# Conditioned residual block on one core: TensorE, VectorE and ScalarE take parts of a step in another order

## The chip, the cores and the metric

The kernel runs on one core of a Trainium2 chip. The time is device microseconds of one launch; the figure for a kernel is the median over its runs.

## The reference, cut to what matters

Two residual layers over x of 2 batches x 2048 rows x 512 features, all float32:

```
x1  = x + x @ W(mu) + bias(mu)      W(mu) = U(mu) @ V, rank 30, one per batch
xn  = norm(x1)                      rows to mean 0, variance 1
h   = norm(xn*pw_g[path] + pw_b[path]) * cp_g[cls] + cp_b[cls]
t   = xn * tm_g[cls] + tm_b[cls]
s   = xn * ms_g[scale] + ms_b[scale]
m,n,r = x1 + three vectors of the batch (from small MLPs of the conditions)
hid = concat(w0 h, w1 t, w2 m, w3 n, w4 r, w5 s) @ int_W1 + b1
y   = x1 + norm(silu(hid) @ int_W2 + b2) * g + be
```

## The kernel before

The 4096 rows are 32 tiles of 128 rows. A head loads and prepares the weights: it decodes U from W_dec, splits every weight into a high part in TensorE's reduced format and the low remainder, and runs the x part of `hid` for twelve tiles (2 to 13, "kept") ahead of time, while W_dec streams in; these results wait in `stash`. Then comes one step per tile.

Each product of 128x512 with a 512x512 weight is three matmuls for each of four chunks (high x high, high x low, low x high), 12 matmuls of 512 columns, in `product` (L743 to L745). What a product needs is first transposed by TensorE (`transpose`, L737, four 128x128 blocks), then copied out of the bank as its high part by ScalarE (`split_hi`, L591) and subtracted for its low part by VectorE (`split_lo`, L1244).

In step n five tiles are in work: a = n+2, f = n+1, m = n, c = n-1, b = n-2. TensorE does, in this order: the x product of m (not for kept tiles, L961), `expand` of f (L804, gives x @ W for x1), the transposes of h of m, `low_rank` of m (L809, the m, n, r parts and the rank part of hid), the t product of m, the transposes of z = silu(hid) of c, the s product of m, the second product of c (with W2, operand `zop`), `offsets` of m (L813, the class offsets by a one-hot matrix), the transposes of t and of s of f, `embed` of a (L794) and the h product of m. A kept step has 51 matmuls of 512 columns, a later one ("ring step", after the ring in which x is loaded) 63.

VectorE sums x1 of f (`first_sum`, L1276), for a kept c adds the stashed x part to hid (L1443, into z), takes x1's statistics (`x_stats`, L1249 and L1253), adds the bias to the output of b and takes its statistics (`out_stats`), multiplies xn by the gains of t (`scaled`, L1288) and s (`scale_rows`, L1296), splits z (`z_split`, L1244), scales the output of b (L1370), splits h, takes h's statistics, finishes b's rows (L1378), splits s, makes the stack for the next expand (`stacked`), the one-hot matrix (L1212), h's class product (`h_gain`, L1305) and splits t. ScalarE applies silu to c (L604 for a kept c, L609 else), makes the high part of x of a (`x_high`, L562), normalises x (`x_norm`, L640), copies z's and h's high parts, then s's, `embedded`, normalises h and copies t's. GpSimd turns variances into factors (L1021, L1029, L1034), subtracts x's low part (`x_low`, L1070), gathers gains by indirect DMA and does h's pathway gain. SyncE issues the loads; for kept tiles x comes to `xraw` (L405).

The order on each engine is written out by hand in the `step` functions; an engine takes its instructions in that order, and the engines meet at semaphores. The steps 15 to 26 are a loop of three rounds of four; the rest is unrolled.

Of the kernel before, what the change touches and what calls it, by code (L numbers as in the profile page):

```python
# [106 lines left out]
def kept(t):  # L107

    return t.i is None and PRE0 <= t.s < PRE0 + NPRE


def ringed(t):

    return t.exists() and not kept(t) and t.s >= PRE0 + NPRE
# [13 lines left out]
def build(nc, d, out):  # L128
# [11 lines left out]
    with ExitStack() as ctx:  # L140
# [369 lines left out]
        def _(act):  # L510
# [40 lines left out]
            def x_high(a):  # L551
                s = a.slot
                old = a.plus(-2)
                if ringed(a):
                    act.wait_ge(stash_in[a.row], ring_count(a))
                    if kept(old):
                        act.wait_ge(xu_ready, old.count())
                    else:
                        act.wait_ge(x_free, old.count())
                else:  # L560
                    act.wait_ge(xT_in[s], a.slot_count(16))
                nc.scalar.activation(xop[:, s, HI, :, :], x_rows(a), ACT.Copy).then_inc(x_hi, 1)  # L562
# [38 lines left out]
            def silu(m):  # L601
                if kept(m):
                    act.wait_ge(z_whole, m.s - PRE0 + 1)
                    nc.scalar.activation(z[:, :], z[:, :], ACT.Silu, bias=0.0).then_inc(z_ready, 1)  # L604
                else:
                    act.wait_ge(hid_ready, m.count())
                    if is_first(m):
                        act.wait_ge(x_used, 1)
                    nc.scalar.activation(z[:, :], HID[m.slot][:, :], ACT.Silu, bias=0.0).then_inc(z_ready, 1)  # L609
# [75 lines left out]

            def step(n):
                a, f, m, c, b = n.plus(2), n.plus(1), n, n.plus(-1), n.plus(-2)
                silu(c)
                if kept(n):
                    x_high(a)  # L690
                if f.exists():
                    x_norm(f)
                z_high(c)
                if m.exists():
                    h_high(m)
                if a.exists() and not kept(n):
                    x_high(a)
                if f.exists():
                    s_high(f)
                if a.exists():  # L700
                    embedded(a)
                if f.exists():
                    h_norm(f)
                    t_high(f)
# [18 lines left out]
        def _(pe):  # L723
# [82 lines left out]
            def low_rank(m):  # L806
                if kept(m):
                    pe.wait_ge(z_ready, m.count(extra=-1))
                return nc.tensor.matmul(HID[m.slot][:, :], stack_of(m), VWst[:, :], start=kept(m), stop=False)  # L809

            def offsets(m):
                pe.wait_ge(oh_ready, m.count())
                nc.tensor.matmul(HID[m.slot][:, :], OH[:, m.slot, :], BT[:, :], start=False, stop=is_first(m)) \  # L813
                    .then_inc(x_used, 1)
# [7 lines left out]
            def transpose_s(m):  # L822
                pe.wait_ge(s_ready, m.count())
                if m.plus(-1).exists():
                    pe.wait_ge(h_lo, m.count(extra=0))
                transpose(TP[1], st, sT)

            def transpose_h(m):
                pe.wait_ge(h_ready, m.count())
                pe.wait_ge(s_lo, m.count())  # L830
                transpose(TP[1], ht, hT)
# [125 lines left out]
            def step(n):  # L957
                a, f, m, c, b = n.plus(2), n.plus(1), n, n.plus(-1), n.plus(-2)
                if m.exists() and not kept(m):
                    pe.wait_ge(z_ready, m.count(extra=-1))  # L960
                    product(HID[m.slot], xop[:, m.slot, :, :, :], W1[:, X, :, :, :], True, False)  # L961
                if f.exists():
                    expand(f)
                if m.exists():
                    transpose_h(m)
                    low_rank(m).then_inc(x_free, 1)
                if kept(m):
                    t_product(m, FRONT)
                if m.exists():
                    t_product(m, BACK if kept(m) else range(KC))  # L970
                transpose_z(c)
                if m.exists():
                    s_product(m)
                if not is_last(m):
                    second_product(c)
                if m.exists():
                    offsets(m)
                if f.exists():
                    transpose_t(f)
                    transpose_s(f)  # L980
                if a.exists():
                    embed(a)
                if m.exists():
                    h_product(m)
# [165 lines left out]
        def _(v):  # L1150
# [107 lines left out]
            def stacked(f):  # L1258
                v.wait_ge(inner_part, f.count())
                nc.vector.tensor_tensor(inner[:, :], inner[:, :], XU[:, P:2 * P], ALU.add).then_inc(inner_ready, 1)  # L1260
                v.wait_ge(inner_ready, f.count())
                if f.plus(-3).exists():
                    v.wait_ge(x_used, f.count(extra=-1))
                dst = stack_of(f)
                nc.vector.tensor_copy(dst[:, :], inner[:, :]).then_inc(stack_part, 1)
                v.wait_ge(stack_part, f.count())
                nc.vector.tensor_tensor(dst[2 * Q:3 * Q, :], inner[2 * Q:3 * Q, :], dst[2 * Q:3 * Q, :].bitcast(F32),
                                        ALU.subtract).then_inc(stack_ready, 1)

            def first_sum(f):  # L1270
                s = f.slot
                v.wait_ge(xv_ready, f.count())
                v.wait_ge(x0_in[s], f.slot_count(16))
                if f.plus(-2).exists():
                    v.wait_ge(xb_ready, f.count(extra=-1))
                nc.vector.tensor_tensor(x1[:, s, :], XV[:, :], x0[:, s, :], ALU.add).then_inc(x1_ready, 1)  # L1276

            def x_stats(f):
                v.wait_ge(x1_ready, f.count())
                stats(0, x1[:, f.slot, :], f, 0, mv1_ready)  # L1280

            def scaled(f):
                m, s = f.plus(-1), f.slot
                v.wait_ge(xhat_ready, f.count())
                v.wait_ge(ct_in[s], f.slot_count(16))
                if m.exists():
                    v.wait_ge(tT, m.count())
                nc.vector.tensor_tensor(tt[:, :], xhat[:, :], ctt[:, s, D:2 * D], ALU.mult).then_inc(t_ready, 1)  # L1288

            def scale_rows(f):  # L1290
                m, s = f.plus(-1), f.slot
                v.wait_ge(xhat_ready, f.count())
                v.wait_ge(sg_in[s], f.slot_count(16))
                if m.exists():
                    v.wait_ge(sT, m.count())
                nc.vector.tensor_tensor(st[:, :], xhat[:, :], sgt[:, s, :], ALU.mult).then_inc(s_ready, 1)  # L1296
# [6 lines left out]
            def h_gain(f):  # L1303
                v.wait_ge(hn_ready, f.count())
                nc.vector.tensor_tensor(ht[:, :], ht[:, :], ctt[:, f.slot, 0:D], ALU.mult).then_inc(h_ready, 1)  # L1305
# [130 lines left out]
            def step(n):  # L1436
                a, f, m, c, b = n.plus(2), n.plus(1), n, n.plus(-1), n.plus(-2)
                if f.exists():
                    first_sum(f)
                if c.exists() and kept(c):  # L1440
                    v.wait_ge(hid_ready, c.count())
                    v.wait_ge(zT, c.count(extra=0))
                    nc.vector.tensor_tensor(z[:, :], HID[c.slot][:, :], stash[:, c.s - PRE0, :],  # L1443
                                            ALU.add).then_inc(z_whole, 1)
                if f.exists():
                    x_stats(f)
                out_stats(b)
                if f.exists():
                    scaled(f)
                    scale_rows(f)  # L1450
                z_split(c)
                out_scaled(b)
                if m.exists():
                    h_split(m)
                if f.exists():
                    h_stats(f)
                out_row(b)
                if f.exists():
                    s_split(f)
                if a.exists():  # L1460
                    stacked(a)
                    one_hot(a)
                if f.exists():
                    h_gain(f)
                    t_split(f)

            for n in range(2, FIRST):
# [133 lines left out]
```

## Time and profile before

| what | value |
|---|---|
| median of 3 runs | 621.7 us (621.47 to 622.83) |
| the profiled execution | 621.03 us |
| its span | 619.2 us |
| PE / PEld busy | 588.5 / 452.8 us |
| DVE / ACT / POOL busy | 418.3 / 200.1 / 391.1 us |
| granted TensorE clock | 0.997 of full speed |

The span is what the trace covers; 1.8 us of the execution lie outside it. PE is TensorE's matmuls, PEld its weight loads, DVE VectorE, ACT ScalarE, POOL GpSimd. Matmuls are pipelined: a matmul's own duration overlaps the next one, so the distance between two starts is what it costs.

### The profile page before, as it was taken

How to read it: one execution, taken by the hardware profiler on the slowest of the kernel's cores; microseconds unless marked ns; L12 is line 12 of the kernel's file. 1: busy time of each engine (PE TensorE's matmuls, PEld its weight loads, DVE VectorE, ACT ScalarE, POOL GpSimd, SP SyncE). 2: the span in 40 equal slices, each digit the busy share in tenths (PEclk: the TensorE clock that was granted, in tenths of full speed). 3: DMA queues.
4: the chain of work that ended last, by engine and by line, in shares of the span. 5: the costliest groups of instructions: out<-in, count | busy, mean ns of one | idle time of the engine just before them, and what ended most of it. 6: DMA issues, size and time to landing. Idle time of an engine off the chain costs nothing.

```text
span 619.2 us, 9159 instructions
## 1 busy us (share of the span) xinstructions
PE 588.5 (95%) x2924; PEld 452.8 (73%) x2924; DVE 418.3 (68%) x750; ACT 200.1 (32%) x346; POOL 391.1 (63%) x499
## 2 busy tenths in 40 slices
PE   0899899999999999999999999999999999999995
PEld 0455346588888888888888888888888888888784
DVE  3511378588888888888676667766666666667744
ACT  3333354433333334333232332333223322332222
POOL 1002457568888888888766766666777666666720
PEclk9999999999999999999999999999999999999998
DMA  8999997424554445545524444454433434444201
GB/s 290 405 403 379 325 344 266 128 87 140 157 158 141 141 148 162 162 153 153 147 100 124 133 141 125 122 140 140 140 123 103 134 121 122 132 140 104 88 19 51
DMA packets 53119, 102.07 MB, mean 165 GB/s; under 512 B 10446, under 2 KB 23246, under 8 KB 52956
## 3 DMA queue, kind: packets, MB, share of 16 engines
q1 hardware_dynamic: 39872, 58.52, 27.7%
q0 software_dynamic: 12160, 42.04, 22.6%
q10 hardware_dynamic: 1052, 1.07, 0.5%
q8 instruction: 18, 0.29, 0.2%
q14 instruction: 17, 0.14, 0.1%
HBM read 93.10 MB, written 8.39 MB: 164 GB/s over the span
## 4 chain that ended last, share of the span: by engine, by line
PE 78%; DMA 6%; DVE 5%; issue 3%; POOL 3%; ACT 2%; SPq 1%; ACTq 0%; DVEq 0%; POOLq 0%
PE bank L743 21%; PE bank L745 21%; PE bank L744 21%; PE bank L737 8%; DMA ring<-in_W_dec 4%; PE bank L794 2%; PE bank L731 2%; SPq L332 1%; DMA Uf<-Ur 1%; PE bank L813 1%; PE bank L809 1%; PE bank L804 1%; DVE bn L1249 1%; POOL rs L1029 1%; DMA pwt<-in_pw,idx 1%
## 5 line engine op out<-in xcount | busy, mean ns | idle before, releaser
L743 PE MATMUL bank<-W,ops 128*128 128x512 f32 x432 | 175.4, 406 | 0.0
L745 PE MATMUL bank<-W,ops 128*128 128x512 f32 x432 | 171.0, 396 | 0.0
L744 PE MATMUL bank<-W,ops 128*128 128x512 f32 x432 | 170.9, 396 | 0.0
L591 ACT ACTIVATE ops<-bank 128x512 fp32r<-128x512 f32 x97 | 57.1, 590 | 158.1 <-PE bank L737 158.1
L743 PEld LDWEIGHTS bank<-W,ops 128*128 128x128 f32 x432 | 81.6, 189 | 25.6 <-issue 8.6
L745 PEld LDWEIGHTS bank<-W,ops 128*128 128x128 f32 x432 | 81.3, 188 | 19.6
L744 PEld LDWEIGHTS bank<-W,ops 128*128 128x128 f32 x432 | 81.6, 189 | 16.1
L1244 DVE TENSOR_TENSOR ops<-bank,ops 128x512 fp32r<-128x512 f32 x97 | 66.2, 683 | 14.1 <-ACT ops L591 14.1
L1249 DVE BATCH_NORM_STATS2 bn<-h 128x6 f32<-128x512 f32 x32 | 22.2, 692 | 55.2 <-POOL h L1081 55.2
L1021 POOL TENSOR_SCALAR ve<-mv 128x1 f32<-128x1 f32 x94 | 31.6, 336 | 42.9 <-DVE mv L1253 40.4
L640 ACT ACTIVATE xhat<-x,nm,rs 128x512 f32<-128x512 f32 x32 | 26.1, 816 | 94.1 <-POOL nm L1034 94.1
L743 PE MATMUL bank<-W,zop 128*128 128x512 f32 x124 | 50.7, 409 | 0.7 <-DVE zop L1244 0.4
L1081 POOL TENSOR_TENSOR h<-h,pwt 128x512 f32<-128x512 f32 x32 | 47.5, 1484 | 2.5
L744 PE MATMUL bank<-W,zop 128*128 128x512 f32 x124 | 49.0, 395 | 0.0
L745 PE MATMUL bank<-W,zop 128*128 128x512 f32 x124 | 48.9, 395 | 0.0
L1070 POOL TENSOR_TENSOR xop<-stash,xop 128x512 fp32r<-128x512 f32 x18 | 23.3, 1293 | 39.4 <-ACT xop L562 39.4
L1370 DVE SCALAR_TENSOR_TENSOR o<-o,mv,gbc 128x512 f32<-128x512 f32 x31 | 47.5, 1531 | 0.0
L1046 POOL DMA_INDIRECT ctt<-in_ct,idx x32 | 40.3, 1258 | 7.7 <-issue 6.4
L1079 POOL TENSOR_TENSOR h<-xhat,pwt 128x512 f32<-128x512 f32 x32 | 42.7, 1334 | 2.9 <-ACT xhat L640 1.9
L647 ACT ACTIVATE ht<-h,nm,rs 128x512 f32<-128x512 f32 x32 | 26.1, 816 | 56.1 <-POOL nm L1034 56.1
L332 POOL DMA_DIRECT2D Uf<-Ur x12 | 6.5, 564 | 58.4 <-ACT Ur L548 58.4
L1090 POOL TENSOR_TENSOR xb<-x,bebc 128x512 f32<-128x512 f32 x32 | 42.3, 1323 | 0.6
(145 smaller groups left out, 1084.5 us busy)
## 6 DMA issues: line engine op xcount, KB each, us to landing
ring<-in_W_dec SPq DMA_DIRECT2D x16, 960.0 KB, 12.1
x<-in_x SPq DMA_DIRECT2D x32, 256.0 KB
out<-xb SPq DMA_DIRECT2D x31, 256.0 KB
stash<-in_xT SPq DMA_DIRECT2D x30, 256.0 KB, 6.2
ring<-in_int_W SPq DMA_DIRECT2D x4, 1024.0 KB, 9.8
xraw<-in_xT SPq DMA_DIRECT2D x14, 256.0 KB
mnr<-in_int_W SPq DMA_DIRECT2D x12, 256.0 KB, 8.2
idxrep<-in_rows SPq DMA_DIRECT2D x64, 32.0 KB
```

What stands on the lines that cost most here:

```text
L591: nc.scalar.activation(dst.rearrange("p c t -> p (c t)"), bank[:, :], ACT.Copy).then_inc(done, 1)
L737: last = nc.tensor.transpose(dst[:, c * P:(c + 1) * P], src[:, c * P:(c + 1) * P], ident)
L743: nc.tensor.matmul(bank[:, :], op[:, HI, c, :], w[:, HI, c, :], start=start and c == 0, stop=False)
L744: nc.tensor.matmul(bank[:, :], op[:, HI, c, :], w[:, LO, c, :], start=False, stop=False)
L745: last = nc.tensor.matmul(bank[:, :], op[:, LO, c, :], w[:, HI, c, :], start=False, stop=stop and c == KC - 1)
L1021: nc.gpsimd.tensor_scalar(ve[:, which:which + 1], mv[:, which, 1:2], EPS, 1.0, ALU.add, ALU.mult) \
L1046: pool.indirect_dma_start(out=dst[:, s, :], out_offset=None, in_=d[table], in_offset=bass.IndirectOffsetOnAxis(ap=idx[:, s, col:col + 1], ...
L1079: nc.gpsimd.tensor_tensor(h1[:, :], xhat[:, :], pwt[:, s, 0:D], ALU.mult).then_inc(h1_part, 1)
L1081: nc.gpsimd.tensor_tensor(h1[:, :], h1[:, :], pwt[:, s, D:2 * D], ALU.add).then_inc(h1_ready, 1)
L1090: nc.gpsimd.tensor_tensor(xb[:, f.row, :], x1[:, f.slot, :], bebc[:, :], ALU.add).then_inc(xb_ready, 1)
L1244: nc.vector.tensor_tensor(dst.rearrange("p c t -> p (c t)"), bank[:, :], hi.bitcast(F32).rearrange("p c t -> p (c t)"), ALU.subtract).then ...
L1370: nc.vector.scalar_tensor_tensor(out=o[:, :], in0=o[:, :], scalar=mv[:, 2, 0:1], in1=gbc[:, :], op0=ALU.subtract, op1=ALU.mult).then_inc(u ...
```

## The change

Nothing is added or removed; instructions change places within the step of three engines. The head written out before the first step, the loads and GpSimd's order stay.

```diff
@@ ScalarE, step @@
-                silu(c)
                 if kept(n):
                     x_high(a)
+                silu(c)
                 if f.exists():
                     x_norm(f)
                 z_high(c)
@@ TensorE, step @@
                 if f.exists():
                     expand(f)
                 if m.exists():
+                    low_rank(m).then_inc(x_free, 1)
                     transpose_h(m)
-                    low_rank(m).then_inc(x_free, 1)
...
                 if not is_last(m):
                     second_product(c)
-                if m.exists():
-                    offsets(m)
                 if f.exists():
                     transpose_t(f)
                     transpose_s(f)
+                if m.exists():
+                    offsets(m)
                 if a.exists():
                     embed(a)
@@ VectorE, step @@
                 if f.exists():
                     first_sum(f)
+                    x_stats(f)
                 if c.exists() and kept(c):
                     v.wait_ge(hid_ready, c.count())
                     v.wait_ge(zT, c.count(extra=0))
                     nc.vector.tensor_tensor(z[:, :], HID[c.slot][:, :], stash[:, c.s - PRE0, :],
                                             ALU.add).then_inc(z_whole, 1)
-                if f.exists():
-                    x_stats(f)
                 out_stats(b)
                 if f.exists():
+                    scale_rows(f)
                     scaled(f)
-                    scale_rows(f)
                 z_split(c)
...
                 if a.exists():
                     stacked(a)
+                if f.exists():
+                    h_gain(f)
+                if a.exists():
                     one_hot(a)
                 if f.exists():
-                    h_gain(f)
                     t_split(f)
```

## Rows read from the trace of the kernel before

**Rows 1.** The page's part 1: busy us, share of the span, instructions.
```profile
PE 588.5 (95%) x2924; PEld 452.8 (73%) x2924; DVE 418.3 (68%) x750; ACT 200.1 (32%) x346; POOL 391.1 (63%) x499
```
**Rows 2.** Busy time by stretch: stretch, its length, engines, clock, DMA share, GB/s.
```profile
200.00:250.00 50.00, 49.92 (x252) 40.50 (x251) 42.51 (x79) 17.45 (x31) 41.43 (x54) 1.00 0.48 151
...
400.00:450.00 50.00, 50.00 (x248) 40.98 (x247) 34.22 (x64) 14.75 (x27) 35.04 (x45) 1.00 0.46 130
```
**Rows 3.** Waits from 143 to 303 us: total us, times, longest.
```profile
PEld bank L743 <- DVE zop L1244: 5.1, 11, 0.5
```
**Rows 4.** Timeline of one kept step, TensorE: start, duration, engine, line, what, count, [idle before].
```profile
215.06 0.39 PE L813 MATMUL bank<-BT,OH 128*128 128x512 f32 x1
...
219.43 0.39 PE L804 MATMUL bank<-Vst,stack 128*128 128x512 f32 x1
...
222.88 0.59 PEld L737 LDWEIGHTS bank<-cst,z 128*128 128x128 f32 x4
...
223.12 0.60 PE L737 MATMUL bank<-cst,z 128*128 128x128 f32 x4
...
226.12 0.40 PE L745 MATMUL bank<-W,ops 128*128 128x512 f32 x1
...
226.56 0.50 PE L743 MATMUL bank<-W,zop 128*128 128x512 f32 x1
...
226.90 0.40 PE L744 MATMUL bank<-W,zop 128*128 128x512 f32 x1
...
229.46 0.40 PE L813 MATMUL bank<-BT,OH 128*128 128x512 f32 x1
```
**Rows 5.** The same step on VectorE, from x1's sum to z's split.
```profile
219.90 0.68 DVE L1276 TENSOR_TENSOR x<-bank,x 128x512 f32<-128x512 f32 x1
...
220.50 0.68 DVE L1443 TENSOR_TENSOR z<-bank,stash 128x512 f32<-128x512 f32 x1
...
221.09 0.69 DVE L1249 BATCH_NORM_STATS2 bn<-x 128x6 f32<-128x512 f32 x1
...
221.89 0.18 DVE L1253 BATCH_NORM_AGGREGATE mv<-bn 128x2 f32<-128x6 f32 x1
...
223.51 0.18 DVE L1253 BATCH_NORM_AGGREGATE mv<-bn 128x2 f32<-128x6 f32 x1
...
224.39 0.91 DVE L1288 TENSOR_TENSOR tt<-xhat,ctt 128x512 f32<-128x512 f32 x1 [0.70 <-ACT xhat L640]
...
225.23 0.68 DVE L1296 TENSOR_TENSOR st<-xhat,sgt 128x512 f32<-128x512 f32 x1
...
225.83 0.68 DVE L1244 TENSOR_TENSOR zop<-bank,zop 128x512 fp32r<-128x512 f32 x1
```
**Rows 6.** The same step on ScalarE and GpSimd, with the wait before each.
```profile
221.21 0.63 ACT L604 ACTIVATE z<-z 128x512 f32<-128x512 f32 x1 [2.15 <-DVE z L1443]
...
221.75 0.61 ACT L562 ACTIVATE xop<-xraw 128x512 fp32r<-128x512 f32 x1
...
222.23 0.19 POOL L1021 TENSOR_SCALAR ve<-mv 128x1 f32<-128x1 f32 x1 [0.48 <-DVE mv L1253]
...
223.55 0.82 ACT L640 ACTIVATE xhat<-x,nm,rs 128x512 f32<-128x512 f32 x1 [1.18 <-POOL nm L1034]
```
**Rows 7.** Timeline of a ring step on VectorE, where statistics follow x1's sum directly.
```profile
410.82 0.69 DVE L1276 TENSOR_TENSOR x<-bank,x 128x512 f32<-128x512 f32 x1 [0.55 <-PE bank L804]
...
411.55 0.70 DVE L1249 BATCH_NORM_STATS2 bn<-x 128x6 f32<-128x512 f32 x1
```
**Rows 8.** Groups by form, 160 to 600 us: busy us, mean ns, idle before.
```profile
L809 PE MATMUL bank<-VWst,stack 128*128 128x512 f32 x28 | 13.3, 475 | 0.0
...
L813 PE MATMUL bank<-BT,OH 128*128 128x512 f32 x27 | 10.6, 393 | 0.0
```
**Rows 9.** SyncE issues the load of x for the kept step.
```profile
217.02 0.43 SPq L405 DMA_DIRECT2D xraw<-in_xT  x1
```
**Rows 10.** DMA issues by line: count, KB each, median us to landing.
```profile
stash<-in_xT SPq DMA_DIRECT2D x30, 256.0 KB, 6.2
```

## The prediction

> **What bounds the kernel now.** I read the page's busy shares first, then the busy time by stretch, then the waits of the stage with the smallest margin, then one step of it on every engine. The shares say TensorE: 588.5 of 619.2 us [rows 1]. The stretches say where it could still gain: from 400 to 450 us, in the ring steps, it is busy 50.00 of 50 us, from 200 to 250 us, in the kept steps, 49.92, with VectorE at 42.5 us and GpSimd at 41.4 [rows 2]. Busy time hides what pipelining costs, so I go by starts. The waits of 143 to 303 us name one thing before the weight loads: `zop`, the low part of z, from VectorE, 11 times [rows 3].
>
> In one kept step the price can be read. Two matmuls of the second product that follow each other are 0.233 us apart. The last matmul of the s product starts at 226.12, the first that needs zop at 226.56, the next at 226.90: 0.78 us where two distances would be 0.47, so 0.31 us are lost, partly in waiting, partly because the weights of the late matmul could no longer be loaded under the one before [rows 4]. The step is 229.46 - 215.06 = 14.40 us long; without the loss it would be 14.09, and nothing else in it waits. A ring step has 12 matmuls more, 12 x 0.233 = 2.8 us in which zop gets ready, and loses nearly nothing.
>
> Why is zop late? z's split is at 225.83, behind the products for t (224.39) and s (225.23) on VectorE; the t product waited 0.70 us for xhat [rows 5]. ScalarE could start xhat only at 223.55, when GpSimd had the factor; GpSimd started at 222.23 on the statistics, which VectorE finished at 221.89 + 0.18 = 222.07 [rows 5, 6]. These statistics stood behind the sum of z with the stash (220.50), which takes VectorE's place for 0.60 us.
>
> **The change part by part.** I count from the start of `expand` of the same step, E = 219.43 [rows 4].
>
> *x's statistics before z's stash sum.* The first statistic starts today at E+1.66. Put directly behind x1's sum it needs that sum's result, and in a ring step this costs 0.73 us from start to start instead of 0.60 [rows 7]: sum at E+0.47, statistic at E+1.20, 0.46 us earlier than now. Everything on that chain moves with it: statistics done at E+2.18, GpSimd's factor begins at E+2.34, xhat at 4.12 - 0.46 = E+3.66 and ready at E+4.48. The work on VectorE between does not get less, only its idle 0.70 us shrinks: the stash sum goes to E+2.10 (0.10 behind the start of x's aggregate at E+2.00), and the output's bias and statistics, whose aggregate ends at 223.51 + 0.18 = E+4.26 now [rows 5], are pushed by the 0.13 us that x's sum and statistic lie further apart, to about E+4.40, just before xhat. So the multiplication that waits for xhat starts at E+4.50, the next after 0.84 (the first of the two takes 0.91 us, as now: GpSimd subtracts x's low part beside it) at E+5.34, z's split after 0.60 at E+5.94, done at E+6.62. z's high part is no obstacle: ScalarE can copy it as soon as xhat is through, at about E+4.4. TensorE wants zop for the matmul at 226.12 + 0.233 = E+6.92, with its weights loaded, for which I take 0.11 us (the excess of 0.34 over 0.233 between 226.56 and 226.90) [rows 4]. The low part reaches it 0.05 after VectorE's end, as today (226.51 to 226.56), so at E+6.67 against E+6.81. The stall of 0.31 us goes, with 0.14 us to spare. What is late next is the stash sum itself.
>
> *The stash sum later, silu later.* It ends at E+2.78 instead of E+1.75, silu (0.63 us) runs from E+2.81 to E+3.44, and the weight load of z's transposes, today at 222.88 = E+3.45, can take it at E+3.49. That is 0.04 late, but a load may start 0.11 before its matmul at E+3.69. So it costs nothing; the margin is under 0.1 us. This is the tightest place. Bounds: 0 if the lead holds, 0.04 to 0.10 a step if not, 0.5 to 1.2 us over twelve steps; I take 0, because the deadline is that of the matmul.
>
> *x's high part before silu on ScalarE.* Today it starts at 221.75 = E+2.32, without any wait for its load, 0.54 us after silu [rows 6]; its load was issued at 217.02 = E-2.41 [rows 9], so the landing takes at most 4.73 us. The issue hangs on the output rows of b, which are on the chain that moves 0.46 earlier while the step gets 0.31 shorter, so it comes at about E-2.56; the latest landing that the trace allows is then E+2.17, x's high part is done by E+2.8 and silu starts at E+2.81 as above. Cost 0, hidden in the wait of 2.15 us that ScalarE has before silu. What it brings is an earlier x_low operand, which nobody waits for.
>
> *s product before t product on VectorE.* Both of t and s are wanted only by the transposes after the second product, three microseconds later. Cost and gain 0.
>
> *h's class product before the one-hot matrix.* In ring steps VectorE idles before it for the normalised h anyway; the 0.29 us of the one-hot matrix then lie behind it and push t's split by up to 0.3, where VectorE afterwards idles 0.55 us [rows 7]. In kept steps t's split keeps its place, as the same work is done before it. Cost 0.
>
> *low_rank before h's transposes, offsets behind those of t and s.* The same matmuls are issued, and there are still three changes from transposes to matmuls in a step. The matmul right behind transposes lasts longer (low_rank 475 ns, offsets, behind a product, 393) [rows 8]: 0.08 us, the part of a weight load that a short transpose cannot cover. After the change the t product's first matmul and offsets stand there instead of low_rank and embed. So the same price is paid in the same number of places. I take 0; the bounds are one such exposure more or less per step, 0.08 x 30 = 2.4 us either way. The h transposes get 0.23 us more time for h; nobody waits for either moved matmul, since both add into an open sum.
>
> No DMA is moved; those of SyncE follow the same semaphores.
>
> **The sum.** Eleven kept steps x 0.31 = 3.4 us [rows 3, 4]. Ring steps, head and tail 0. The profiled execution goes from 621.03 to 617.6 us (span 619.2 to 615.8); it lies 0.7 us under the median, so the median goes from 621.7 to 618.3 us.
>
> **The rivals.**
>
> *A: silu is held up behind x's load (slower).* ScalarE takes its instructions in order. If x's load has not landed, silu waits with it, and TensorE waits at z's transposes. The median landing of the same 256 KB into stash is 6.2 us [rows 10]. At that, x lands at E+3.64, silu ends near E+4.9 and the transposes stall by about 1.4 us, in the nine kept steps (3 to 11) whose x comes through xraw: 9 x 1.4 = 12.6 us more, less the 3.4 us of the zop stall that goes, so about 631 us. It decides from a landing of 5.2 us on (x at E+2.64, silu and z 0.45 later than in my count, 0.31 us of stall behind the lead: all the gain). For it: order, and that median. Against it: all those landings took at most 4.73 us, or x's high part would have shown a wait [rows 6, 9]. The Trainium skill ("TensorE: Matmul & The Clock Gate", section "Architectural detail: the array is 16× 32×32, not 1× 128×128") says that ScalarE's and VectorE's queues are strictly first in, first out, and only weight loads are pulled ahead. The trace agrees: z's split stood behind the t product that waited 0.70 us [rows 5]. By that rule rival A has no way out once a load is late.
>
> *B: the stall only moves (no change).* The margins of 0.14 us at zop and below 0.1 at z's transposes are both differences of overlapping spans. If the stash sum, 0.9 us later than now, makes z's transposes late by 0.1 to 0.2 us, and zop is late by as much, a step keeps most of its 0.31 us: 620.0 to 621.5 us, I say 620.7. For it: VectorE's work ahead of z's split is unchanged and only 0.70 us idle can be taken from it. Against it: the counts above.
>
> The Trainium skill ("SBUF — State Buffer", section "SBUF: two separate sides") has VectorE and GpSimd lock each other out of a shared port for a whole instruction when VectorE reads two SBUF operands. The t product's 0.91 us while x_low ran fits that more or less. By the rule the first product would wait for x_low's end at about E+4.89, zop would come 0.15 us later than in my sum, and the gain would be some 0.1 us smaller in all.
>
> *C: TensorE's new neighbours cost or save an exposed weight load in each of 30 steps.* 618.3 + 2.4 = 620.7, or 618.3 - 2.4 = 615.9 us. Rows 8 speak for a fixed price per change of kind, so for neither.
>
> **How the numbers follow.** Forecast 0.66, A 0.08, B 0.14, C dearer 0.05, C cheaper 0.05, and 0.02 for slower in another way. The range takes B and the dearer C in and reaches 1.5 us below the forecast: 616.8 to 621.0; outside remain A, most of the cheaper C and little else. About 0.2%, 1.2 us, is what a measurement can tell here: faster is below 620.5, which has the forecast, the cheaper C and some of B and the dearer C, 0.79; within 0.2% the rest of these, 0.11; slower A and the rest, 0.10.
>
> **What would show it.** Right: in the kept steps no wait of the weight loads for zop, steps of 14.1 us between two `offsets`, x's statistic 0.73 us behind x1's sum, xhat 0.46 us earlier after expand, silu ending about 3.4 us after expand with z's transposes still at 3.7, ring steps unchanged at 16.9. Wrong: a wait of z's transposes for silu (B, or A if x's high part shows a wait for its load); ring steps shorter or longer by 0.08 (C).

## The result, and the profile after

The changed kernel runs in 618.68 us (median of 6, 618.12 to 619.33) against 622.12 us (median of 6) for the kernel before on the same chip: ratio 0.9946, 95% interval 0.9933 to 0.9959. That is 3.4 us less; the forecast was 3.4 us less and 618.3 us. A run that lies over 1.5% above the fastest of its kernel is left out of medians and ratios; in this document that is one run, of e9. The two profiled executions differ by 2.0 us only (spans 619.2 and 617.2 us), since in the second one the head, which waits for weights, happened to take 1.1 us longer: `expand` of step 3 starts at 148.51 us there and at 147.41 us before (in the traces of the experiments it lies anywhere from 147.9 to 150.4). From that point on the changed kernel takes 468.7 us and the old one 471.8, 3.1 us less. It lies in the eleven steps from there to `expand` of step 14: 161.26 us before, 158.10 now. A ring step is as long as before, 16.91 us against 16.90.

The page's busy line for the changed kernel [rows 1]:

```profile
PE 586.1 (95%) x2924; PEld 454.5 (74%) x2924; DVE 417.5 (68%) x750; ACT 204.2 (33%) x346; POOL 390.1 (63%) x499
```

The waits of the changed kernel from 143 to 303 us [rows 3]: the eleven waits for zop (5.1 us) are one of 0.2 us, and ScalarE now waits for x's load before it makes x's high part, which before it never did.

```profile
ACT xop L562 <- DMA xraw<-in_xT: 7.0, 9, 1.5
...
ACT xhat L640 <- POOL nm L1034: 2.5, 11, 0.3
...
PEld bank L743 <- DVE zop L1244: 0.2, 1, 0.2
```

TensorE in one kept step of the changed kernel [rows 4]; here E, the start of `expand`, is 219.09:

```profile
215.52 0.47 PE L813 MATMUL bank<-BT,OH 128*128 128x512 f32 x1
...
219.09 0.39 PE L804 MATMUL bank<-Vst,stack 128*128 128x512 f32 x1
219.33 0.39 PE L809 MATMUL bank<-VWst,stack 128*128 128x512 f32 x1
...
222.79 0.60 PE L737 MATMUL bank<-cst,z 128*128 128x128 f32 x4
...
225.79 0.40 PE L745 MATMUL bank<-W,ops 128*128 128x512 f32 x1
226.03 0.39 PE L743 MATMUL bank<-W,zop 128*128 128x512 f32 x1
226.26 0.40 PE L744 MATMUL bank<-W,zop 128*128 128x512 f32 x1
...
229.62 0.47 PE L813 MATMUL bank<-BT,OH 128*128 128x512 f32 x1
```

The first matmul that needs zop starts 0.24 us after the one before and its follower 0.23 us later, where both together took 0.78 us. The step is 14.10 us long. `low_rank`, no longer behind transposes, shows 0.39 us and `offsets`, now behind them, 0.47: the exposed weight load changed its place, as rows 8 had it.

VectorE in the same step [rows 5]: x's statistic at E+1.19, aggregate at E+1.99, stash sum at E+2.09, then s, t and z's split.

```profile
219.57 0.68 DVE L1276 TENSOR_TENSOR x<-bank,x 128x512 f32<-128x512 f32 x1
220.28 0.69 DVE L1249 BATCH_NORM_STATS2 bn<-x 128x6 f32<-128x512 f32 x1
221.08 0.18 DVE L1253 BATCH_NORM_AGGREGATE mv<-bn 128x2 f32<-128x6 f32 x1
221.18 0.69 DVE L1444 TENSOR_TENSOR z<-bank,stash 128x512 f32<-128x512 f32 x1
...
223.64 0.91 DVE L1296 TENSOR_TENSOR st<-xhat,sgt 128x512 f32<-128x512 f32 x1 [0.15 <-ACT xhat L640]
224.47 0.68 DVE L1288 TENSOR_TENSOR tt<-xhat,ctt 128x512 f32<-128x512 f32 x1
225.07 0.68 DVE L1244 TENSOR_TENSOR zop<-bank,zop 128x512 fp32r<-128x512 f32 x1
```

ScalarE and GpSimd in it [rows 6]: x's high part is done before silu may start, and nothing stands before xhat but GpSimd's factor.

```profile
220.07 0.63 ACT L562 ACTIVATE xop<-xraw 128x512 fp32r<-128x512 f32 x1 [1.45 <-DMA xraw<-in_xT]
...
221.91 0.64 ACT L604 ACTIVATE z<-z 128x512 f32<-128x512 f32 x1 [1.21 <-DVE z L1444]
...
222.72 1.28 POOL L1070 TENSOR_TENSOR xop<-xraw,xop 128x512 fp32r<-128x512 f32 x1
222.79 0.81 ACT L640 ACTIVATE xhat<-x,nm,rs 128x512 f32<-128x512 f32 x1 [0.25 <-POOL nm L1034]
```

### The profile page after: what moved, and what is told of

Same layout as the page of the kernel before. It is cut to its first block, busy times and chain, and to the rows that moved or that the text cites. A ratio compares the mean times of both kernels' runs of the same rounds, so it can differ in the third digit from the quotient of the medians.

```text
span 617.2 us, 9159 instructions
## 1 busy us (share of the span) xinstructions
PE 586.1 (95%) x2924; PEld 454.5 (74%) x2924; DVE 417.5 (68%) x750; ACT 204.2 (33%) x346; POOL 390.1 (63%) x499
## 4 chain that ended last, share of the span: by engine, by line
PE 68%; POOL 7%; issue 7%; DMA 7%; DVE 6%; SPq 2%; ACT 2%; POOLq 0%; DVEq 0%; ACTq 0%
PE bank L743 18%; PE bank L744 18%; PE bank L745 18%; PE bank L737 7%; DMA xraw<-in_xT 2%; PE bank L731 2%; DMA ring<-in_W_dec 2%; DMA ring<-in_int_W 2%; PE bank L794 2%; SPq L332 2%; DVE bn L1249 2%; POOL rs L1029 1%; POOL h L1081 1%; POOL h L1079 1%; POOL ctt L1046 1%
## 5 line engine op out<-in xcount | busy, mean ns | idle before, releaser
L744 PEld LDWEIGHTS bank<-W,ops 128*128 128x128 f32 x432 | 81.9, 190 | 14.8
L1046 POOL DMA_INDIRECT sgt<-in_ms_g,idx x32 | 35.4, 1105 | 11.4 <-issue 11.4
## 6 DMA issues: line engine op xcount, KB each, us to landing
ring<-in_W_dec SPq DMA_DIRECT2D x16, 960.0 KB, 12.5
```

The lines of the kernel that those rows point to most:

```text
L744: nc.tensor.matmul(bank[:, :], op[:, HI, c, :], w[:, LO, c, :], start=False, stop=False)
L1046: pool.indirect_dma_start(out=dst[:, s, :], out_offset=None, in_=d[table], in_offset=bass.IndirectOffsetOnAxis(ap=idx[:, s, col:col + 1], ...
```

## The experiments

Each is given with its median and its ratio to the kernel before on the same chip. All expectations count from E, as the prediction does. The third column of the table is the mean length of the eleven steps from `expand` of step 3 to that of step 14 in the trace, less the 2.80 us that the x product (12 matmuls) puts into the last of them; it leaves the head's scatter out. Single slow steps are in these means: one of 14.86 us in e1, of 14.40 in e2 and of 15.19 in e3; the medians of the eleven are 14.40, 14.10 and 14.56.

| kernel | median us, ratio (95% interval) | kept step us |
|---|---|---|
| before | 622.1 | 14.41 |
| changed | 618.68, 0.9946 (0.9933 to 0.9959) | 14.12 |
| e1, statistics only | 621.82, 0.9996 (0.9987 to 1.0005) | 14.46 |
| e2, statistics and x's high part | 619.33, 0.9954 (0.9940 to 0.9967) | 14.14 |
| e3, all but the statistics | 623.54, 1.0020 (1.0011 to 1.0029) | 14.60 |
| e5, x's high part only | 621.69, 0.9996 (0.9986 to 1.0007) | 14.40 |
| e6, TensorE's moves only | 622.07, 1.0000 (0.9992 to 1.0009) | 14.38 |
| e7, e3 with the one-hot matrix back | 622.58, 1.0008 (0.9998 to 1.0018) | 14.40 |

**e1, x's statistics before z's stash sum, nothing else.**

```diff
                 if f.exists():
                     first_sum(f)
+                    x_stats(f)
                 if c.exists() and kept(c):
...
-                if f.exists():
-                    x_stats(f)
                 out_stats(b)
```

> Before, with x's statistics put before z's stash sum on VectorE and nothing else. Theory 1, as the prediction had it (x's high part before silu is worth nothing): the whole stall at zop goes, 3.4 us faster than before, the same as the full change. Theory 2: with silu now at E+2.8 to E+3.45, x's high part, which stands behind silu here, runs until about E+4.0 and holds xhat back from E+3.7 to about E+3.9; zop comes some 0.25 us later than in the changed kernel and the matmul waits 0.1 to 0.15 us more in each kept step: only about 2 us faster than before.

Measured 621.82 us: no gain at all, less than even the second theory gave. E is 221.96 in this step of e1:

```profile
224.75 0.63 ACT L604 ACTIVATE z<-z 128x512 f32<-128x512 f32 x1 [3.18 <-DVE z L1444]
225.29 0.62 ACT L562 ACTIVATE xop<-xraw 128x512 fp32r<-128x512 f32 x1
225.81 0.80 ACT L640 ACTIVATE xhat<-x,nm,rs 128x512 f32<-128x512 f32 x1
...
225.99 1.29 POOL L1070 TENSOR_TENSOR xop<-xraw,xop 128x512 fp32r<-128x512 f32 x1 [0.36 <-ACT xop L562]
...
226.65 1.18 DVE L1288 TENSOR_TENSOR tt<-xhat,ctt 128x512 f32<-128x512 f32 x1 [0.32 <-ACT xhat L640]
...
228.36 0.68 DVE L1244 TENSOR_TENSOR zop<-bank,zop 128x512 fp32r<-128x512 f32 x1
```

Silu waits for the later stash sum and x's high part, behind it, holds up two things: xhat starts at E+3.85 where the changed kernel has E+3.70, and GpSimd's x_low at E+4.03 where it has E+3.63. The t product, which overlaps x_low, then lasts 1.18 us; in the changed kernel the first product lasts 0.91. Of the 0.42 us by which z's split was early in the changed kernel (E+5.98 against E+6.40 before), nothing is left: E+6.40. About 0.15 us of it went with xhat, 0.27 us with the longer product.

**e2, the same with x's high part before silu.** e1 and, on ScalarE:

```diff
-                silu(c)
                 if kept(n):
                     x_high(a)
+                silu(c)
```

> Before, with x's statistics before the stash sum and x's high part before silu, TensorE's order and the rest of VectorE's as before. Both theories: 3.4 us faster than before, equal to the full change. If TensorE's moves or h's class product matter (rival C or a tighter chain of h), it stays behind the full change by 0.5 us or more.

619.33 us, and kept steps of 14.14 us: the whole gain within the intervals. Two of the six moves make the change; what the other four add to it is below what these intervals can tell, about 1 us.

**e3, the changed kernel with the statistics back behind the stash sum.**

```diff
                     first_sum(f)
-                    x_stats(f)
                 if c.exists() and kept(c):
...
+                if f.exists():
+                    x_stats(f)
                 out_stats(b)
```

> The changed kernel with x's statistics put back behind the stash sum. Theory (the stall at zop hangs on xhat, and xhat on the statistics): xhat again at E+4.1, 0.31 us lost in each of eleven kept steps, the time of before within 0.5 us. Rival (the other moves each bring something): 1 us or more faster than before.

Slower than before, 623.54 us, neither theory's number. The stall at zop is there in all eleven steps and bigger. The step of e3 with E = 223.80 on VectorE:

```profile
222.98 0.69 DVE L1305 TENSOR_TENSOR ht<-ht,ctt 128x512 f32<-128x512 f32 x1 [0.39 <-ACT ht L647]
223.59 0.28 DVE L1212 TENSOR_SCALAR OH<-idxrep,cst 128x128 fp32r<-128x128 int32 x1
...
224.39 0.68 DVE L1276 TENSOR_TENSOR x<-bank,x 128x512 f32<-128x512 f32 x1
```

VectorE idles 0.39 us for the normalised h and does the one-hot matrix afterwards, which before filled that gap; x1's sum starts at E+0.59 instead of E+0.47, and everything on the way to zop with it.

**e7, e3 with the one-hot matrix ahead of h's class product again.**

```diff
                 if a.exists():
                     stacked(a)
-                if f.exists():
-                    h_gain(f)
-                if a.exists():
                     one_hot(a)
                 if f.exists():
+                    h_gain(f)
                     t_split(f)
```

> The kernel with all edits but the statistics (e3, 623.5 us, x1's sum at E+0.59 instead of E+0.47), with the one-hot matrix put back ahead of h's class product. Theory: in e3 VectorE idled 0.39 us before h's product and then had 0.2 us of the one-hot matrix to do behind it, which pushed t's split and x1's sum by 0.12 us in each kept step: with it back, x1's sum at E+0.47 and the time of before (622.2), 1.3 us under e3. Rival (TensorE's or ScalarE's move costs the 1.3 us): stays at 623.5.

622.58 us with kept steps of 14.40 instead of 14.60: back to before within the interval, as expected. So this one move of the change costs about 1 us where the statistics are late (0.7 by the ratios, 1.0 by the medians). The intervals of e3 and e7 overlap a little; what carries the finding is the step, whose median is 14.56 us in e3 and 14.38 in e7. In the changed kernel h's normalised rows come earlier, x1's sum starts at E+0.48, and it costs nothing.

**e5, x's high part before silu, nothing else** (e2's ScalarE edit on the kernel before).

> Before, with x's high part before silu on ScalarE and nothing else. Theory (the position counts only where xhat is wanted early): x's high part ends at about E+1.7 instead of E+2.9, silu and xhat stay where they are (statistics late, xhat at E+4.1), so the time of before within 0.5 us. Rival (it helps by itself through x_low or frees ScalarE for xhat): 1 us or more faster.

621.69 us, ratio 0.9996: nothing, as expected. The two moves that make the gain are each worth nothing alone.

**e6, TensorE's two moves, nothing else.**

```diff
                 if m.exists():
+                    low_rank(m).then_inc(x_free, 1)
                     transpose_h(m)
-                    low_rank(m).then_inc(x_free, 1)
...
-                if m.exists():
-                    offsets(m)
                 if f.exists():
                     transpose_t(f)
                     transpose_s(f)
+                if m.exists():
+                    offsets(m)
```

> Before, with TensorE's two moves only (low_rank before h's transposes, offsets behind those of t and s). Theory: the exposed 0.08 us only change their place, the time of before within 0.5 us. Rival C: 2.4 us slower or faster.

622.07 us, ratio 1.0000 (0.9992 to 1.0009): rival C is out, in both directions.

**e4, z's split between t's and s's product, in the kernel before.**

```diff
                     scaled(f)
-                    scale_rows(f)
                 z_split(c)
+                if f.exists():
+                    scale_rows(f)
```

> Before, with z's split between the t and the s product on VectorE, statistics where they were. Theory (only the time at which zop is ready counts, not why): z's split starts about 0.84 us after the t product at E+5.8, so zop is ready at E+6.5 and the matmul loses nothing: 3.4 us faster than before, although xhat comes no earlier. Rival (it is the earlier statistics that help, through GpSimd's chain or h): same as before.

630.74 us, ratio 1.0143 (1.0128 to 1.0159): 8.6 us slower. The wait for zop is gone from TensorE, but nine of the eleven kept steps take 15.3 to 15.7 us. One of these on VectorE, GpSimd and TensorE:

```profile
217.26 2.27 DVE L1296 TENSOR_TENSOR st<-xhat,sgt 128x512 f32<-128x512 f32 x1
...
217.66 1.31 POOL L1079 TENSOR_TENSOR h<-xhat,pwt 128x512 f32<-128x512 f32 x1
...
219.04 1.64 POOL L1081 TENSOR_TENSOR h<-h,pwt 128x512 f32<-128x512 f32 x1
...
219.45 1.79 DVE L1370 SCALAR_TENSOR_TENSOR o<-o,mv,gbc 128x512 f32<-128x512 f32 x1
...
221.98 0.63 PE L737 MATMUL bank<-cst,st 128*128 128x128 f32 x4 [0.72 <-DVE ops L1244]
```

The s product lasts 2.27 us instead of 0.68: it meets GpSimd's first product for h and ends 0.56 us after it (217.66 + 1.31 = 218.97, 217.26 + 2.27 = 219.53). The scaling of the output behind it then meets GpSimd's second one and ends 0.56 us after that one (220.68, 221.24). VectorE is 1.6 us behind, h's split late, and s's transposes wait for it. The other two kept steps show that this is the cause: in them the s product keeps its 0.68 us (at 247.99 and 278.19), and they take 14.47 and 14.46 us.

**e8, the same in the changed kernel.**

```diff
                     scale_rows(f)
-                    scaled(f)
                 z_split(c)
+                if f.exists():
+                    scaled(f)
```

> The changed kernel with z's split between the s and the t product on VectorE. Theory P (e4 lost 8.6 us because its s product began just as GpSimd began h's first product and stood 2.27 us instead of 0.68): here the t product, last of the three, starts at about E+6.0, 0.4 us before GpSimd's product at E+6.4, takes 0.7 us, and the time is that of the changed kernel within 0.5 us (618.7), with zop ready 0.6 us earlier. Rival (a multiplication behind z's split delays out_scaled and the rest of the step in itself): 5 us or more slower than the changed kernel, as in e4.

627.60 us, ratio 1.0097 (1.0084 to 1.0110), 9 us slower than the changed kernel. My theory P had the meeting right and its outcome wrong: the t product starts 0.41 us before GpSimd's instruction and still stands 2.24 us. The same happens in nine of the eleven kept steps, which take 14.8 to 15.2 us; in the other two the t product keeps 0.67 and 0.68 us (at 245.71 and 275.29), and they take 14.44. Of the 0.3 us that these still have over the changed kernel, most is lost at their start, where TensorE waits for a split that the long step before them made late.

```profile
230.64 2.24 DVE L1288 TENSOR_TENSOR tt<-xhat,ctt 128x512 f32<-128x512 f32 x1
...
231.05 1.28 POOL L1079 TENSOR_TENSOR h<-xhat,pwt 128x512 f32<-128x512 f32 x1
```

**e9, the changed kernel with x's load issued later.**

```diff
-                if kept(a):
-                    load_x(a)
                 if a.exists():
                     load_rows(a)
+                if kept(a):
+                    load_x(a)
```

> The changed kernel with the load of x for kept tiles issued behind the four loads of rows and indices in SyncE's step, some 2.5 us later. In the changed kernel it landed at about E+1.0, so here at E+3.5. Theory (rival A of the prediction, in-order ScalarE): x's high part runs E+3.5 to E+4.1, silu to E+4.75, z's transposes wait 1.2 us in each of the nine kept steps whose x is loaded so: 11 us slower than the changed kernel, about 629 us. Other theory (the wait has slack elsewhere, GpSimd and VectorE set the step): under 3 us slower.

633.39 us (median of 3, 631.03 to 635.81), ratio 1.0162 (1.0126 to 1.0197), 13 us slower than the changed kernel by the ratios and 15 by the medians. In the step with E = 229.58 the load is issued at 228.74, lands 4.8 us later, at E+3.95, and z's transposes wait:

```profile
228.74 0.58 SPq L405 DMA_DIRECT2D xraw<-in_xT  x1
...
233.53 0.63 ACT L562 ACTIVATE xop<-xraw 128x512 fp32r<-128x512 f32 x1 [4.86 <-DMA xraw<-in_xT]
...
234.73 0.66 PE L737 MATMUL bank<-cst,z 128*128 128x128 f32 x4 [1.30 <-ACT z L604]
```

That is rival A's mechanism. It is real: in eight of the nine steps z's transposes start 1.60 to 2.53 us after the matmul before, where 0.23 is usual, so 1.4 to 2.3 us are lost; the prediction's 1.4 us is the low end. (In the ninth x's high part began at E+1.09 and nothing was lost.) The 11 us expected were short because the load was late by more than E+3.5: in those eight steps x's high part begins at E+3.86 to E+4.79. It did not happen in the changed kernel because there x's high part could begin at E+0.98 at the latest, and at E+0.11 to E+0.39 in the other eight steps.

**e10, the kernel before with the same later load** (the same edit).

> Before with the same later load. There silu stands ahead of x's high part, so z's transposes are on time; x's high part ends at E+4.1 and xhat is held back by at most a few tenths of a us (E+4.1 to E+4.2 or so). Theory: 0 to 3 us slower than before, far less than the 11 us that the same delay costs the changed kernel. Other theory (a late load costs the same wherever its reader stands): 11 us slower.

634.48 us, ratio 1.0201 (1.0168 to 1.0234), 12.5 us slower than before. My expectation was wrong. z's transposes are on time in all steps but one, but x's high part stands before xhat here, and the step (E = 224.82) loses about as much at zop:

```profile
229.37 0.63 ACT L562 ACTIVATE xop<-xraw 128x512 fp32r<-128x512 f32 x1 [2.15 <-DMA xraw<-in_xT]
229.91 0.81 ACT L640 ACTIVATE xhat<-x,nm,rs 128x512 f32<-128x512 f32 x1
...
233.19 0.50 PE L743 MATMUL bank<-W,zop 128*128 128x512 f32 x1 [1.26 <-DVE zop L1244]
```

So a late load is no argument for either order: with silu first it hits xhat, with x's high part first it hits silu.

## Why the prediction was right, and where it was not

*The bound and the stall.* TensorE was the bound, and 0.31 us per kept step at zop was all that could be had. Measured: 14.41 to 14.12 us, 0.29 us. The rest is a few hundredths of a us in some of the steps.

*The statistics.* x's statistic was forecast at E+1.20, the stash sum at E+2.10, silu at E+2.81, xhat at E+3.66, the first product at E+4.50, z's split at E+5.94. The trace has 1.19, 2.09, 2.82, 3.70, 4.55 and 5.98. z's transposes start at E+3.70 with no wait but one of 0.2 us in eleven steps (rival B in a single step). The mechanism and the sizes of this step stand.

*x's high part before silu.* This is the part that the prediction had wrong. It put the move at 0 and said that what it brings is an x_low operand that nobody waits for. e1 and e2 show 2.5 us between them (621.82 and 619.33 us): without this move the earlier statistics are worth nothing, since x's high part then runs at E+3.33 to E+3.95, in xhat's way (0.15 us) and before x_low, whose end the first product has to outlast (0.27 us more). Nobody waits for the operand, but the subtraction that makes it holds up VectorE. The sum came out right because it counted xhat with x's high part already out of the way, and both moves were in the change; which of them earns the gain, and that neither does alone, was not foreseen. I had followed what the move delays (silu) and not what would stand at its old place once silu is 0.9 us later.

*s before t.* Nothing measured speaks against the 0; it was not undone alone. It is in e3 and e7, and e7 is the time of before.

*h's class product before the one-hot matrix.* Right for the changed kernel, with x1's sum at E+0.48. Not free in itself: e3 against e7, 0.2 us in a typical step of the traces and 1 us in the medians, when h's rows come late.

*TensorE's moves.* 0, as forecast (e6).

*The range of A.* The prediction bounded the landing by 4.73 us from the issue. The changed kernel shows it: issue at 216.58 in the trace, x's high part begins at 220.07, 3.5 us. That is the longest of the nine; the others take 2.6 to 2.9 us. There was over a microsecond of room more than the bound gave, and the median of 6.2 us of the loads into stash was no guide to these.

*The port.* The prediction weighed a rule of the Trainium skill ("SBUF — State Buffer", section "SBUF: two separate sides") by which VectorE and GpSimd lock each other out for a whole instruction. The durations agree with a lock. Where GpSimd has the port, a VectorE multiplication with both operands in SBUF that meets a GpSimd tensor instruction ends 0.54 to 0.56 us after that instruction, however long it has then stood: 0.91 us beside x_low in the changed kernel (222.72 + 1.28 = 224.00, 223.64 + 0.91 = 224.55), 1.18 in e1 (227.28, 227.83), 2.27 in e4 and 2.24 in e8. By the rule the prediction had z's split 0.15 us later than in its sum; it came 0.04 later (E+5.98 against E+5.94), because the multiplication that was let in late needed 0.55 us more and not its usual 0.68.

The same section of the Trainium skill says that the one that starts first gets the port. By the recorded starts this holds in some steps and not in others. It holds in all 32 ring steps of e4 and e8: VectorE's multiplication starts 0.12 to 0.37 us before x_low and keeps its 0.68 us, and x_low, else 1.3 us, takes 1.46 to 1.72. One of them, of e4:

```profile
410.01 0.68 DVE L1296 TENSOR_TENSOR st<-xhat,sgt 128x512 f32<-128x512 f32 x1
...
410.25 1.59 POOL L1070 TENSOR_TENSOR xop<-stash,xop 128x512 fp32r<-128x512 f32 x1 [2.58 <-ACT xop L562]
```

It does not hold in the kept steps shown of e4 and e8, where the multiplication starts 0.40 and 0.41 us before GpSimd's product and loses. There GpSimd comes from its gather without a pause (the gather ends 0.04 us before the product starts), while in the ring steps it had stood idle. That GpSimd claims the port some 0.4 us ahead of its recorded start when it does not pause would fit both, and also the one kept step of e8 where the multiplication starts 0.52 us ahead and wins (275.29); one step of e4 with 0.40 us (278.19) goes the other way than its nine neighbours. No run tests this.

## What to carry to other kernels

When an instruction is moved on an in-order engine, follow also the ones that keep their places: ask what now stands before the operand that ends last, once the moved one's inputs come later. Two moves can each measure zero and make the whole gain together, so undo parts singly and in pairs before dropping one. Before a multiplication whose operands both lie in SBUF is moved on VectorE, look at what GpSimd runs at its new place.

## What the hardware showed that I had not expected

A single 512-column multiplication of VectorE can take 2.27 us instead of 0.68 by its place alone (e4); in nine kept steps this cost 8.6 us over the kernel. The same 256 KB were in use 2.6 to 2.9 us after the issue (once 3.5) when issued ahead of the loads of rows and indices, and 4.2 to 5.6 us after it, mostly 4.7 to 5.0, behind them (e9). In the two steps shown, issuing the load 1.7 us later (E-0.84 instead of E-2.51) made it 3 us later.
